# Layer 0 of a two-layer cross-attention kernel: normalised sums on GpSimd, query columns in single PSUM banks, and paced transfers

## The reference

```
# layer 0: 8 groups of key/value heads, 4 query heads in each, head width 16
q = x @ Wq + bq;  k = c @ Wk + bk;  v = c @ Wv + bv
scores = einsum('bkgld,bksd->bkgls', q, k) / sqrt(16) + mask    # mask: 512 x 1024 per entry
attn = softmax(scores, axis=-1)
out = einsum('bkgls,bksd->bkgld', attn, v)  -> 512 x 512
x = layernorm(out @ Wo + bo + x) * gamma + beta
# layer 1: twice x += cross_attention(layernorm(x), c) with 16 heads of width 128 and one bias
# key and value; then x + gelu(layernorm(x) @ W1 + b1) @ W2 + b2
```

## Time and profile before

| what | value |
|---|---|
| median of three executions | 2584.71 us (2584.61 to 2585.48) |
| profiled execution, its own time | 2584.9 us |
| span of its trace | 2583.1 us |
| busy share of the span: PE, DVE, ACT, POOL | 97%, 66%, 58%, 51% |
| layer 0 of entry 0 | about 0 to 290 us |
| layer 0 of entry 1 | about 1300 to 1573 us |
| chain that ended last | PE 80%, DVE 12%, issue 3%, the rest 1% or less each |

### The profile page before, as it was taken

One profiled execution on the slowest core, in us unless ns is written; L12 is line 12 of the kernel. 1 busy time (PEld: TensorE's weight loads), 2 busy tenths in 40 slices (PEclk: granted clock), 3 DMA queues, 4 the chain that ended last, 5 costly groups with the idle time before them and its releaser, 6 DMA issues.

```text
span 2583.1 us, 53124 instructions
## 1 busy us (share of the span) xinstructions
PE 2501.0 (97%) x19500; PEld 2067.1 (80%) x19500; DVE 1704.7 (66%) x2600; ACT 1496.1 (58%) x2360; POOL 1312.1 (51%) x746
## 2 busy tenths in 40 slices
PE   7999999999999999999989999999999999999999
PEld 6666688888888888888866667888888888888877
DVE  6999666566656656665269996656665675666541
ACT  5999455555445555545459994555555555554553
POOL 1154346665544666555602443566556456655644
PEclk8999999999999999999989999999999999999999
DMA  7222044454414445442462220445445144544522
GB/s 208 79 71 83 34 100 100 119 133 106 121 55 100 100 116 130 112 117 68 155 157 68 79 70 34 100 114 129 115 116 124 36 100 110 131 117 112 126 72 65
DMA packets 86915, 263.60 MB, mean 102 GB/s; under 512 B 20544, under 2 KB 26320, under 8 KB 81120
## 3 DMA queue, kind: packets, MB, share of 16 engines
q1 hardware_dynamic: 85760, 260.80, 38.4%
q10 hardware_dynamic: 992, 0.52, 0.1%
HBM read 135.39 MB, written 8.40 MB: 56 GB/s over the span
## 4 chain that ended last, share of the span: by engine, by line
PE 80%; DVE 12%; issue 3%; POOL 1%; ACT 1%; DMA 1%; SPq 1%; DVEq 0%; POOLq 0%; ACTq 0%
PE ps_m L1091 21%; PE ps_t L1091 19%; PE ps_s L1091 17%; DVE sm L1695 7%; PE ps_m L1355 7%; PE ps_t L1355 6%; PE ps_s L1212 4%; DVE pt L1703 2%; POOL pT_lo L557 1%; PE ps_m L1288 1%; PE ps_m L1101 1%; PE ps_m L1246 1%; SPq L470 1%; DVE nm L1695 1%; PE ps_t L1229 1%
## 5 line engine op out<-in xcount | busy, mean ns | idle before, releaser
L557 POOL TENSOR_TENSOR pT_lo<-pT_lo,pT_hi 128x1024 fp32r<-128x1024 f32 x220 | 529.9, 2409 | 498.2 <-ACT pT_hi L743 486.8
L743 ACT ACTIVATE pT_hi<-pT_lo 128x1024 fp32r<-128x1024 f32 x224 | 237.8, 1061 | 327.1 <-DMA pT_lo<-pb 327.1
L882 ACT ACTIVATE p<-ps_s,nm 128x1024 f32<-128x1024 f32 x256 | 285.0, 1113 | 206.0 <-DVE nm L1772 205.6
L1769 DVE TENSOR_REDUCE nmx<-ps_s 128x1 f32<-128x1024 f32 x256 | 309.6, 1209 | 122.0 <-PE ps_s L1091 122.0
L1091 PE MATMUL ps_s<-kT,qT 128*128 128x512 f32 x1536 | 384.2, 392 | 0.0
L1788 DVE STREAM_TRANSPOSE pb<-p 128x1024 f32<-128x1024 f32 x224 | 278.0, 1241 | 106.7 <-ACT p L882 102.8
L1091 PEld LDWEIGHTS ps_s<-kT,qT 128*128 128x128 f32 x1536 | 281.2, 188 | 55.7 <-ACT p L882 1.3
L835 ACT ACTIVATE p<-sm,nm 128x1024 f32<-128x1024 f32 x256 | 293.3, 1146 | 23.5 <-DVE nm L1695 19.3
L1695 DVE CUSTOM_DVE_ANT_0 sm<-ps_s,mask 128x1024 f32<-128x1024 f32 x256 | 300.8, 1210 | 6.9 <-PE ps_s L1212 5.1
L1091 PE MATMUL ps_t<-ctxT,wa 128*128 128x512 f32 x1080 | 255.9, 390 | 0.0
L1091 PE MATMUL ps_m<-hT,wa 128*128 128x512 f32 x1008 | 243.8, 393 | 0.7 <-ACT g L1053 0.7
(11 more groups left out here) (177 smaller groups left out, 4651.3 us busy)
## 6 DMA issues: line engine op xcount, KB each, us to landing
pT_lo<-pb SPq DMA_DIRECT2D x896, 128.0 KB, 2.3
stg_qk<-in_wqk SPq DMA_DIRECT2D x40, 1024.0 KB, 7.5
stg_vo<-in_wo SPq DMA_DIRECT2D x48, 512.0 KB, 3.6
wob<-in_wo SPq DMA_DIRECT2D x32, 512.0 KB, 3.6
stg_vo<-in_wv SPq DMA_DIRECT2D x32, 512.0 KB, 3.7
q_stack<-scr_q SPq DMA_DIRECT2D x36, 128.0 KB, 4.3
st_ctx<-in_ctxT SPq DMA_DIRECT2D x8, 512.0 KB, 6.0
mask<-in_mask SPq DMA_DIRECT2D x8, 512.0 KB, 5.9
```

The costliest lines, as they stand in the source:

```text
L557: return nc.gpsimd.tensor_tensor(out, x, f32(hi), ALU.subtract)
L743: return nc.scalar.activation(out, in_, ACT.Copy)
L882: nc.scalar.activation(p[t % 2][:], ps_s[t % 2][:], ACT.Exp, bias=nm[:, i:i + 1], scale=SCALE1, accum_out=sums[:, i:i + 1]).then_inc(exp_d ...
L1769: nc.vector.tensor_reduce(nmx[:, i:i + 1], ps_s[t % 2][:], AX.X, ALU.max, negate=True)\
```

## The change

It does six things. (1) `normalised` moves from DVE to POOL. ACT's copy now takes all 256 columns (sums and reciprocals) instead of 128, into SBUF, and POOL multiplies the two halves of rb0. PE now waits for ACT's copy (rb0_done) instead of the product (a0_done) before it writes the next unit's sums. (2) The query columns 2 and 3 go to the single banks ps_m[0] and ps_m[1], so that scores may start when four of the six parts have left their banks; column 3 is projected between the first and the second scores, its `wide` stands between the first two `exp0`, its `low_part` behind the fourth `maxima0`. (3) The values' low passes go ahead of query column 0. (4) On SP the stacks and mask tiles of columns 1 to 3 are spread: for column i, scr_q waits for group 1, 3, 6; q_stack and mask tile i + 1 for group 1, 4, 7; the keys' share for group 2, 5, 8. (5) x_res, acc and wob wait for groups five later than before. (6) `value_rows` runs two in each of units 8 to 15, and POOL's row addition waits until unit 7.

```diff
-ROWS_OF_UNIT = (0, 0, 0, 0, 0, 1, 2, 1, 2, 1, 2, 1, 2, 1, 2, 1)
+ROWS_OF_UNIT = (0, 0, 0, 0, 0, 0, 0, 0, 2, 2, 2, 2, 2, 2, 2, 2)
...
-        rb0 = sb("rb0", [P, P], F32, 2)
+        rb0 = sb("rb0", [P, 2, P], F32, 2)
...
         bank0 = [ps_m[0][:], ps_m[1][:], ps_s[0][:, 0:512], ps_s[1][:, 0:512],
-                 ps_s[0][:, 512:1024], ps_s[1][:, 512:1024]]
+                 ps_m[0][:], ps_m[1][:]]
...
                 for i in range(4):
-                    if i >= 2:
-                        after_group(i - 1)
+                    if i >= 1:
+                        after_group(3 * i - 3 if i > 1 else 1)
                     sp.wait_ge(part_done, b * 6 + i + 3)
                     sp.dma_start(scr_q[i, :, :, :], f32(parts[(i + 2) % 3][:])).then_inc(scr_q_out, 16)
...
                     if i == 0:
                         stack_q(0, stack_in, slice(0, P))
                         stack_q(0, stack_next, slice(P, L))
+                        load_mask(1)
                     else:
-                        stack_q(i, stack_rest)
-                    if i < LT - 1:
-                        load_mask(i + 1)
-                    if i == 1:
+                        after_group(3 * i - 2)
+                        stack_q(i, stack_rest[i - 1])
+                        if i < LT - 1:
+                            load_mask(i + 1)
+                        after_group(3 * i - 1)
                         for k in range(2):
-                            sp.wait_ge(scr_k_out[k], 16 * (b + 1))
-                            apart()
-                            stack_k(sp, k, slice(1, KVP), stack_rest)
+                            stack_k(sp, k, slice(i, i + 1), stack_rest[i - 1])
 
                 for lt in range(LT):
-                    after_group(4 + lt)
+                    after_group(9 + lt)
...
-                after_group(8)
+                after_group(13)
...
                     if f < 2:
-                        after_group(9 + f)
+                        after_group(14 + f)
...
+                def normalised(u):
+                    kp, lt = divmod(u, LT)
+                    pool.wait_ge(rb0_done, u0 + u + 1)
+                    nc.gpsimd.tensor_tensor(aT0[:, kp, lt * P:(lt + 1) * P], rb0[u % 2][:, 0, :], rb0[u % 2][:, 1, :],
+                                            ALU.mult).then_inc(a0_done, 1)
+
                 for u in range(UNITS0):
-                    if u == 4:
+                    if u == 7:
...
                         .then_inc(r0_done, 1)
+                    if u >= 1:
+                        normalised(u - 1)
+                normalised(UNITS0 - 1)
...
-                for i in range(3, 6):
+                for i in range(3, 5):
                     wide(b, i)
...
+                def sums_out(u):
+                    act.wait_ge(rb0_filled, b * UNITS0 + u + 1)
+                    if u >= 2:
+                        act.wait_ge(a0_done, b * UNITS0 + u - 1)
+                    copy(rb0[u % 2][:], unit_inverse0(u).rearrange("p (x n) -> p x n", x=2)).then_inc(rb0_done, 1)
+
                 exp0(0)
+                wide(b, 5)
                 exp0(1)
...
-                        act.wait_ge(rb0_filled, b * UNITS0 + u + 1)
-                        copy(rb0[u % 2][:], inverse0(u)).then_inc(rb0_done, 1)
+                        sums_out(u)
...
+                for i in range(2):
+                    finish_v(i)
                 pe.wait_ge(x_lo, 2 * b + 2)
                 pe.wait_ge(w0q_lo, CT * b + 1)
                 project_q0(0)
-                for i in range(2):
-                    finish_v(i)
...
-                for i in range(2, 4):
-                    pe.wait_ge(w0q_lo, CT * b + i + 1)
-                    project_q0(i)
+                pe.wait_ge(w0q_lo, CT * b + 3)
+                project_q0(2)
...
-                pe.wait_ge(bank_free, nb + U_PROJ0 + 2)
+                pe.wait_ge(bank_free, nb + P_Q[2] + 2)
...
+                        elif bank_of_half[2 * t + q] == 2:
+                            pe.wait_ge(bank_free, nb + U_PROJ0 + 2)
...
-                        pe.wait_ge(a0_done, u0 + u)
+                        pe.wait_ge(rb0_done, u0 + u)
...
                 scores0(0)
+                pe.wait_ge(w0q_lo, CT * (b + 1))
+                project_q0(3)
                 scores0(1)
...
-                for i in range(3, 6):
+                for i in range(3, 5):
                     low_part(i)
...
-                def normalised(u):
-                    kp, lt = divmod(u, LT)
-                    dve.wait_ge(rb0_done, u0 + u + 1)
-                    nc.vector.tensor_tensor(aT0[:, kp, lt * P:(lt + 1) * P], unit0(u), rb0[u % 2][:],
-                                            ALU.mult).then_inc(a0_done, 1)
...
+                    if t == 1:
+                        low_part(5)
                     copied0(t - 1, 1)
                     copied0(t, 1)
-                    if t % UNIT == GROUPS - 1 and t > UNIT:
-                        normalised(t // UNIT - 1)
```

More of the change, by code:

```diff
@@ L223, in build @@
         scr_k_out, scr_q_out = [sem(f"scr_k_out{i}") for i in range(2)], sem("scr_q_out")
-        stack_in, stack_next, stack_rest = sem("stack_in"), sem("stack_next"), sem("stack_rest")
+        stack_in, stack_next, stack_rest = sem("stack_in"), sem("stack_next"), [sem(f"stack_rest{k}") for k in range(1, KVP)]
         out_done = sem("out_done")
@@ L309, in inverse0, with unit_inverse0 @@
             return ps_m[0][:, u % 2 * 2 * P + P:u % 2 * 2 * P + 2 * P]
+        def unit_inverse0(u):
+            return ps_m[0][:, u % 2 * 2 * P:u % 2 * 2 * P + 2 * P]
         def turned_in(x, q, lt):
@@ L858, in batch @@
                         exp0(t + 2)
-                act.wait_ge(rb0_filled, b * UNITS0 + UNITS0)
-                copy(rb0[1][:], inverse0(UNITS0 - 1)).then_inc(rb0_done, 1)
+                sums_out(UNITS0 - 1)
                 act.wait_ge(row_added, b * ROWS + 2)
@@ L1168, in project_q0 @@
                         pe.wait_ge(batch_done, b + 1)
+                    if i >= 2:
+                        free(nb + i)
                     for c in range(CT):
@@ L1263, in _ @@
                         pe.wait_ge(stack_next, 16 * 6 * (b + 1))
-                    if r + 1 == PAIRS0 // KVP:
-                        pe.wait_ge(stack_rest, 16 * 30 * (b + 1))
+                    if (r + 1) % (PAIRS0 // KVP) == 0 and r + 1 < PAIRS0:
+                        pe.wait_ge(stack_rest[(r + 1) // (PAIRS0 // KVP) - 1], 16 * 18 * (b + 1))
                     if r + 1 < PAIRS0:
```

1 line of the change is left out of this document (removed).

## The result

| | before | after |
|---|---|---|
| median of 20 executions each | 2585.81 us (2582.68 to 2591.11) | 2589.09 us (2585.57 to 2593.41) |
| ratio to before | 1 | 1.0014, 95% interval 1.0008 to 1.0020 |
| profiled execution | 2584.9 us (span 2583.1) | 2591.31 us (span 2589.0) |

The changed kernel is slower by 0.14%, 3.3 us by the medians: less than the 0.2% taken as the bound of a difference, but on the other side than forecast, and its time lies above the range of 2571 to 2586. The two profiled spans are 5.9 us apart.

A forecast was written before the change was run, and what follows sets the result against it. DVE, busy 100.00 of 100 us mid-loop, was taken as the bound. Wins of 5.6, 5.3 and 4.8 us less 9.4 lost gave 6.3 us off the profiled 2584.9, stated as 2578.5 us; range 2571 to 2586.

The forecast's parts named there:

- Term 1: Layer 0 loop: `normalised` leaving DVE wins 0.20 us a unit, 5.6 us in all; ACT's and POOL's extra work hidden.
- Term 2: Start of layer 0: first scores come earlier, 3.2 us in entry 0 and 2.1 in entry 1, 5.3 won.
- Terms 3 and 4: Start of layer 0's loop: column 3 there loses 0.8 us, contained in the first 16 steps' net 4.8 us won.
- term 4: First 16 steps of layer 0: 31.8 us from first scores to step 16's maxima in each entry, 4.8 us won.
- Term 5: Step 24: DVE waits 3.6 us for mask tile 3, plus 1.1 at low clock; 9.4 us lost over both entries.
- Rival A: Step 24: mask tile 3 is not late, so its 9.4 us loss is gone, 2569.1 us; chance 0.17.
- Term 6: Layer 0's later x_res, acc, wob and rows: cost nothing, or at most one row, 4.6 us, if late.
- Rival B: First 16 steps no faster: step 7's stall comes from a fixed-place instruction fetch, column 3 and tile 2 eat the rest; 2583.3 us, chance 0.20.
- Rival C: Groups 1 to 8: transfer bursts meeting instruction fetches cost 4.3 us each, three hits give 2591.4 us, slower; chance 0.08.

The follow-up runs named there:

- e7: Changed kernel plus 24 unread identity transposes on PE ahead of the wait for q_stack; 2587.35 us, ratio 1.0013 to the kernel before.
- e2: Changed kernel with query column 3 projected ahead of the first scores, masks still late; 2583.81 us, ratio 1.0002 to the kernel before.
- e10: Kernel before with only the paced SP queue, later x_res, acc and wob, and the new rows of units; 2591.56 us, ratio 1.0025.
- e4: Kernel before with the keys' share of k_stack issued behind column 3's q_stack instead of column 1's; 2579.05 us, ratio 0.9988.
- e1: Changed kernel with mask tile 2 issued at group 1 ahead of scr_q, tile 3 at group 2 ahead of the keys' share; 2581.33 us, ratio 0.9987 to before.
- e5: Changed kernel with mask tiles 2 and 3 at groups 1 and 2 and column 3 ahead of the first scores; 2576.77 us, ratio 0.9964 to before.
- e8: Changed kernel with column 3 before scores, values' low passes behind column 0, before's times for scr_q, q_stack and masks, only keys' shares late; 2573.58 us, ratio 0.9957 to before.

## Why the prediction was wrong

**Term 1, `normalised`: right in kind, 0.16 and not 0.20 a unit.** The start-to-start reading of the earlier trace rows missed that the next maxima begins a little later behind a copy too. Over 28 units that is 4.5 us instead of 5.6. The balance shows 3.4 from step 32 on; the 0.6 for the two units of each entry ahead of it (4 x 0.16) is hidden in the stretch before. ACT's copy of 256 columns takes 0.36 us (predicted 0.37) and POOL's product 0.46 (0.40), both hidden.

**Term 2, earlier first scores: 4.4 won, 5.3 forecast.** Scores at 31.42 (forecast 31.1); in entry 1 1.5 us won instead of 2.1. The transfer took over as the limit, as said. I named it and did not ask what PE does meanwhile.

**Terms 3 and 4, the failed step.** The balance lies 12.2 us above the forecast (+5.9 against -6.3), and 7.7 of them are here. "I put the maxima of step 4 at 9.3 us from the first scores" rested on "Its projection takes 2.96 us on PE". Step 4 came at 10.81 and 12.96, because those matmuls ran at a granted clock of 0.63 and 0.52: 5.2 us over both entries. I had applied the clock to the wait for tile 3 and, in this term, left 1.5 us for "the short idle times at the start", though making the scores wait for a transfer is what makes that time long. e7 shows it: with PE kept busy the projection takes 3.06 us, and the maxima of step 4 come 9.36 and 9.27 us from the first scores, the forecast's 9.3. So the work was priced right, and its clock was not. e2 shows that one line's place avoids it. The other half of the step is "Any wait is inside the 1.5": tile 2 made DVE wait 2.31 and 0.43 us. In entry 0 it was issued 7.6 us behind scr_q, 1.1 sooner than on the same sequence before (8.7), but took 6.8 us to land and not the 5.1 of the earlier trace rows. This wait differs between executions with the same queue order: 2.31 and 0.43 us in after, 2.06 and none in e10, none and 1.33 in e2, 0.38 and none in e7. So 2.7 us is what this execution paid, and more than most. From step 4 to step 16, without these waits, it took 22.5 and 22.3 us, as forecast (30.3 + 1.5 - 9.3 = 22.5). 5.2 + 2.7 less those 0.2 is the 7.7 us by which term 4 missed.

**Term 5, mask tile 3 late: right, and the largest term.** 3.97 us of waiting in each entry, forecast 3.6; from the first q_stack issue to the landing 9.0 us in entry 0, forecast 9.0. What follows at low clock (0.76 and 0.71 us of gaps at transposes, and slower instructions in the pass between) costs 1.36 and 1.23 more, forecast 1.1. That is 10.5 us against 9.4. The stretch of the balance holds 10.9 plus the 0.6 of term 1, 1.0 more than this, because it also has what follows tile 2's wait at low clock. Rival A, the tile not late, is ruled out.

**Term 6:** nothing seen; behind the loop after is 0.4 us longer than before in entry 0 and 0.5 shorter in entry 1.

**Rival B, the start no faster,** names the right outcome and the wrong reason. "The stall of step 7 comes from the fetch of an instruction block at a fixed place of the code" is half of it: the block is at a fixed place, but in after, e4 and e10 PE goes past it without a stop. The start was no faster because column 3 and tile 2 used up what the stall gave back. That a fetch is mostly hidden, as the Trainium skill has it (Runtime: NRT & Kernel Launch, Instruction fetch mechanics), holds in e4 at this block and not before, where PE stopped 3.18 us; between these two runs only the time of other transfers differs. **Rival C, bursts that meet a fetch,** is not what made after slower: its loop has no gap over 0.8 us that column 3, a mask tile or the clock doesn't explain. But stops of this kind are real in the neighbours: in e1, e5 and e8 PE stops for 1.32 to 2.66 us without a releaser, in e1 and e8 while a burst of q_stack is under way, in e5 while one of k_stack is. The loops of the 13 traces hold 13 such stops of over 1 us, step 7's among them, and each has a packet of 16 KB on the instruction queue q8 that starts between 1.2 us ahead of the stop and 0.3 us behind its begin. About 36 such packets pass in each loop, so most of them stop nothing, also with the data queue full (e4 from 60 to 61 us). And the packet need not meet a backlog: at e1's stop at 59.48 us the data queue has 5.1% in the us of the fetch, and the burst follows. (DMA queues of e1 from 58 to 59 us.)

```profile
q8 instruction: 1, 0.02, 5.8%
q1 hardware_dynamic: 8, 0.02, 5.1%
```

So a fetch and a burst close to each other go with every stop, and what decides between a stop and none stays open.

**In ratios:** `normalised` alone -0.11%, pacing alone +0.25%, and after is at +0.14%. If the parts add up, banks, column 3 and values together gave 0.00%, with an uncertainty of 0.15% or 4 us either way, where the forecast had 5.3 us for the earlier scores.

## What to carry to other kernels

When a wait is moved from one releaser to another, price what stands right behind it at the clock that an idle PE leaves, and put no long PE work on the critical path there; filler or another order avoids it. Pace what can be late (the keys, needed from step 32 on), and not what shares the queue with the next deadline: issuing the keys last was worth 0.12% by itself, the whole pacing scheme cost 0.25%. When a large edit nets nothing, test its parts: here the best mix of them was half a per cent faster than either kernel.
